# Issuing each matmul of the row maxima twice in an attention and mixture-of-experts block

## The reference

```python
q, k = _apply_rope(q, k)                                  # [8, 16, 256, 64]
scores = jnp.einsum('bhqd,bhkd->bhqk', q, k) * scale
attn = jax.nn.softmax(scores, axis=-1)
out = jnp.einsum('bhqk,bhkd->bhqd', attn, v)
...
x = _layernorm(x + attention(x))
x = _layernorm(x + experts(x))
```

## Time and profile before

| | |
|---|---|
| Median of 3 runs | 293.36 us (292.1 to 294.01) |
| Profiled execution, whole | 295.25 us |
| Span of the profiled execution, first to last instruction | 293.5 us |
| Mean granted TensorE clock in the profile | 0.819 |
| Busy in the span | PE 246.1 us, DVE 235.9 us, ACT 168.0 us, PEld 139.2 us, POOL 20.6 us |
| Matmuls | 1785, of them 256 of the row maxima (L353) |

### The profile page before, as it was taken

The page is one execution under the profiler, slowest core; times in us unless marked ns, Lnnn a source line. Parts: engine busy times, 40 slices in busy tenths (PEclk is TensorE's granted clock), DMA queues, the critical chain, the costliest instruction groups (busy, mean ns, idle before and its releaser), DMA issues.

```text
span 293.5 us, 5981 instructions
## 1 busy us (share of the span) xinstructions
PE 246.1 (84%) x1785; PEld 139.2 (47%) x1785; DVE 235.9 (80%) x688; ACT 168.0 (57%) x327; POOL 20.6 (7%) x34
## 2 busy tenths in 40 slices
PE   2737999997789789979988797999799938899991
PEld 0111345464446444645555355546545725466671
DVE  5898786969996989699798969897985794656985
ACT  3901556676858575846677574858534645545210
POOL 5000000000000000000000000000080010000121
PEclk9999999999955965685597859558855797999997
DMA  7153113030302021111113030303120000000012
GB/s 276 59 135 72 37 36 75 1 74 2 74 22 54 22 53 29 43 36 36 45 27 72 1 72 1 72 1 72 27 47 1 0 4 0 2 0 2 36 40 71
DMA packets 20438, 12.66 MB, mean 43 GB/s; under 512 B 2732, under 2 KB 19396, under 8 KB 20420
## 3 DMA queue, kind: packets, MB, share of 16 engines
q1 hardware_dynamic: 20420, 12.44, 16.5%
HBM read 2.92 MB, written 1.05 MB: 14 GB/s over the span
## 4 chain that ended last, share of the span: by engine, by line
issue 71%; PE 17%; DVE 7%; ACT 2%; POOL 2%; POOLq 0%; DVEq 0%
PE ps_o L487 4%; PE ps_s L461 3%; PE ps_t L370 2%; PE ps_s L353 2%; POOL sd L742 1%; PE ps_t L471 1%; PE ps_o L385 1%; PE ps_o L485 1%; ACT hg L715 1%; PE ps_m L448 1%; DVE qk L778 1%; DVE qk L777 1%; ACT oT_sb L651 1%; POOL rs L764 1%; PE ps_m L395 1%
## 5 line engine op out<-in xcount | busy, mean ns | idle before, releaser
L812 DVE TENSOR_REDUCE row_max<-ps_s 128x2 bf16<-128x512 f32 x128 | 86.7, 679 | 20.9 <-PE ps_s L353 19.7
L656 ACT ACTIVATE probs<-ps_t 128x512 bf16<-128x512 f32 x128 | 74.6, 606 | 35.4 <-PE ps_t L370 35.0
L353 PE MATMUL ps_s<-qk 64*128 64x256 bf16 x256 | 67.5, 359 | 7.5 <-DMA qk<-roped 4.8
L370 PE MATMUL ps_t<-qk 128*128 128x256 bf16 x256 | 66.5, 355 | 3.5 <-DMA qk<-mT_sb 1.7
L638 ACT ACTIVATE raw<-ps_m,bqk 128x256 bf16<-128x256 f32 x128 | 51.2, 478 | 9.3 <-PE ps_m L338 5.4
L385 PE MATMUL ps_o<-v_sb,probs 128*128 128x65 bf16 x512 | 46.5, 224 | 3.7 <-DVE o_sb L834 3.2
L385 PEld LDWEIGHTS ps_o<-v_sb,probs 128*128 128x128 bf16 x512 | 41.0, 121 | 16.2 <-issue 5.9
L645 ACT CAST v_sb<-ps_m 128x512 bf16<-128x512 f32 x32 | 17.5, 590 | 47.1 <-PE ps_m L345 47.1
L338 PE MATMUL ps_m<-in_b 128*128 (+1 forms) x128 | 35.3, 396 | 7.8 <-DMA in_b<-in_packed_b 4.6
L370 PEld LDWEIGHTS ps_t<-qk 128*128 128x128 bf16 x256 | 16.5, 106 | 42.3 <-issue 26.1
L834 DVE TENSOR_TENSOR o_sb<-ps_o,r_sum 128x256 bf16<-128x256 f32 x64 | 26.4, 412 | 0.1
(11 more groups left out here) (105 smaller groups left out, 222.7 us busy)
## 6 DMA issues: line engine op xcount, KB each, us to landing
qk<-roped SPq DMA_DIRECT2D x128, 64.0 KB, 2.1
out<-y_sb SPq DMA_DIRECT2D x3, 256.0 KB, 2.1
in_b<-in_packed_b SPq DMA_DIRECT2D x1, 706.0 KB, 5.9
in_f<-in_packed_f SPq DMA_DIRECT2D x1, 586.0 KB
in_b<-in_packed_b SPq DMA_DIRECT2D x1, 516.0 KB, 3.8
in_b<-in_packed_b SPq DMA_DIRECT2D x1, 512.0 KB, 4.7
x_sb<-in_x SPq DMA_DIRECT2D x1, 512.0 KB, 6.7
qk<-mT_sb SPq DMA_DIRECT2D x16, 4.0 KB, 1.7
```

The lines of the kernel that those rows point to most:

```text
L353: mm = nc.tensor.matmul(ps_s[h % 2][:, t * S:t * S + S], qk[0:DH, u % 4, 0, h, t * P:t * P + P], qk[0:DH, u % 4, 1, h, :], start=True, sto ...
L370: mm = nc.tensor.matmul(ps_t[h % 2][:, c * S:c * S + S], qk[:, u % 4, 1, h, c * P:c * P + P], qk[:, u % 4, 0, h, :], start=True, stop=True)
L656: nc.scalar.activation(probs[:, h % 4].rearrange("p c s -> p (c s)"), ps_t[h % 2][:], ACT.Exp, scale=DH ** -0.5).then_inc(exp_done, 1)
L812: nc.vector.tensor_reduce(row_max[:, u % 2, h, :], ps_s[h % 2][:].rearrange("p (t s) -> p t s", s=S), AX_X, ALU.max, negate=True).then_inc ...
```

## The change

Each head's pair of matmuls for the row maxima is issued twice, one pair behind the other, with the same operands and into the same place of the same bank. The signal to DVE is raised by the last matmul of the second pair. Each matmul starts its own accumulation (`start=True`), so the values in the bank are the same.

```diff
+MAX_TIMES = 2
...
                 need(pe, max_done, n(it, UH, u, h - 1))
-                for t in range(QT):
-                    mm = nc.tensor.matmul(ps_s[h % 2][:, t * S:t * S + S],
-                                          qk[0:DH, u % 4, 0, h, t * P:t * P + P],
-                                          qk[0:DH, u % 4, 1, h, :], start=True, stop=True)
+                for _ in range(MAX_TIMES):
+                    for t in range(QT):
+                        mm = nc.tensor.matmul(ps_s[h % 2][:, t * S:t * S + S],
+                                              qk[0:DH, u % 4, 0, h, t * P:t * P + P],
+                                              qk[0:DH, u % 4, 1, h, :], start=True, stop=True)
                 mm.then_inc(s_ready, 1)
```

## The result

| | before | changed |
|---|---|---|
| Median | 293.69 us (292.1 to 294.05, 4 runs) | 298.29 us (296.5 to 300.86, 4 runs) |
| Ratio | | 1.0174, 95% interval 1.0089 to 1.0259 |
| Profiled execution, whole / span | 295.25 / 293.5 us | 300.86 / 299.0 us |
| Mean clock as the profile gives it | 0.819 | 0.895 |
| Matmuls of the maxima | 256 | 512 |

What follows compares the result with a forecast made beforehand. TensorE was taken to bound the kernel at the low clock, VectorE at the high one. With the clock division unchanged, 4.0 + 7.7 + 23.0 = 34.7 us on the 293.36 us median gave 328 us, range 306 to 350, chance 0.72.

Steps and rivals of the forecast that it cites:

- What bounds the kernel: Whole span: TensorE sets the time at the low clock, VectorE at the high one; 0 to 64.1 us taken as low.
- The price of a matmul: Each added maxima matmul of 256 columns on 64 rows: 0.213 us at the low clock, 0.11 at the high.
- Up to 34 us: Start of the kernel, 26 maxima matmuls, partly hidden in PE's waits for DVE: 4.0 us, between 1.5 and 5.5.
- 34 to 64.1 us and the low stretches: PE full, nothing hidden: 36 matmuls cost 7.7 us, then 108 in seven low-clock stretches after 64.1 us cost 23.0.
- The signs that the prediction named: Clock checks: first rise no earlier than 74 us; mean clock far from 0.70, first rise to last maxima, would be wrong.
- I set the net at 0: Clock division between high and low: the change's opposing effects cancel, so 0 us, with bounds 307 and 347 us.
- the two pulls: Added 64-row work delays rises by diluting 128-row work at low clock, and makes falls rarer by filling PE's idle time.
- The falls: Clock drops after PE's 1.76 us wait for DVE's `attn`: rarer with idle time filled, but that wait stays.
- High stretches at 0 us: High-clock stretches after 64.1 us: 87 added matmuls covered by PE's slack under DVE, 0 us, upper bound 9.6.
- Rival 2: Clock stays high once risen because added matmuls fill PE's idle time, kernel gets faster: 286 us, chance 0.08.
- half of the low work turns high: Lower bound of the clock term, after 64.1 us: gives back half of 23.0 + 18.9, 21 us, for 307 us.
- Rival 1: Clock stays low nearly throughout, with low stretches further diluted by 64-row work: 368 us, chance 0.16.

Runs made afterwards that it cites:

- both doubled: Scores and maxima matmuls both issued twice per head, against the kernel before: 287.1 us, ratio 0.9795.
- the kernel on 128 rows: Kernel before with its maxima matmuls run once, on 128 rows in place of 64, added rows nearly all zeros: 273.41 us, ratio 0.9368.

## Why the prediction was wrong

- **What bounds the kernel: right.** TensorE at the low clock, VectorE at the high one; only the runs with three pairs and with both doubled, which load PE far more, make it pace at the high clock as well. So was reading the start as low clock against its column.
- **The price of a matmul: right.** 213 and 110 ns were forecast, 0.43 and 0.21 us per pair measured, eight added matmuls cost 1.7 us between 34 us and the second transposition of maxima, and the run with three pairs gives 196 ns.
- **Up to 34 us: mis-sized.** I took 4.0 us, between 1.5 and 5.5, and 2.3 were measured. More of it hid in PE's waits than I took.
- **34 to 64.1 us and the low stretches, 7.7 + 23.0 us: this is the step that failed.** The price was multiplied by the matmuls that ran low *before*. In the changed kernel 148 issued ones run low, so 74 added ones, 15.8 us instead of 36 for 170. The sum assumed a fixed division between clock levels, though it is made by the very stream that the change thickens. The signs that the prediction named went against it: the first rise came at 38.0 us and not at 74 or later, and the mean clock was 0.88 and not 0.70.
- **"I set the net at 0": wrong, and on evidence that I misread.** The run with three pairs, with its late rise and its long high stretch, fits the two pulls. But their sizes differ. I held that rises would come at transposes or at the output projection. The first rise of the changed kernel has maxima, scores and projections ahead of it, no more. I argued from the 30 us of full PE at the low level that maxima do not help; in a second profile of the same kernel that stretch ended at 59.2 us, and in one whose program agrees to there, at 37.5. One execution had shown the late end of a wide spread.
- **The falls: half right.** The wait for `attn` remains (7.8 us in all against 9.1). But I concluded that the falls behind it would remain as well. With more matmuls around it, a stretch of 71.7 us outlives three closings.
- **High stretches at 0 us: right for a PE with slack, too low here.** 12.6 us per unit against 12.2 (of the kernel on 128 rows, which also lacks the switches) is 0.4 us for 16 added matmuls of 1.7 us. Over the nine or so units at the high clock that makes 3 to 4 us; the forecast allowed up to 9.6.
- **Sum of what was found.** 15.8 us at the low clock less the 3.2 that the start hid (5.5 less 2.3), and 3 to 4 at the high: about 16 us of cost. The two spans differ by 5.5. So about 11 us came back from the clock. This last figure is a remainder; no run measures it by itself.
- **Rivals.** Rival 2 had the right direction (its clock that is never lowered did not come, and the kernel was not faster), the chance 0.08 and a price for its full form only. What happened lies between it and the forecast, and no case of mine had a price there: the bound for "half of the low work turns high" was 307, too high. It counted only low work behind 64.1 us, while here the first rise came 26 us earlier, and it took 4.0 us for the start. The rule of the Trainium skill behind that rival ("TensorE: Matmul & The Clock Gate", section "Why this matters for your kernels": keep TensorE busy to have the full clock) goes the right way in this trace but does not say all that counts: the run on 32 rows kept PE full for 27.3 us and had the low clock, the one on 128 rows left a third of PE idle for 116.1 us and had the high one. Rival 1 happened to neither profile; its dilution fits the first 96.9 us of the run with three pairs.

## What to carry to other kernels

Where TensorE changes between its two clock levels, don't price added or removed matmuls at the present division: ask what they do to the clock, and look at more than one execution, for the places of the changes move. Here added matmuls on 64 rows gave back less of the clock than as many on 128. If spare rows can be given values that don't change the result, such as zeros, try the matmul on all 128: here that took 6.3% off the kernel with no added matmul, by the higher clock and by the switches saved together.

## What the runs showed of the hardware

- At equal matmuls, columns and switches, the added matmuls on 128 rows (scores twice) left 48.2 us at the low clock, those on 64 rows (the change) 99.4 and 87.2. With the added pairs on 32 rows it is 153.8, with all maxima twice on 128 rows 28.5; these two also differ in their switches.
- Rows of zeros do not keep the clock down: the kernel on 128 rows has its high clock with 63 of the 64 added rows zero. Whether they count as much as others no run shows.
- PE busy for 65% of 116.1 us kept the full clock (maxima on 128 rows); PE busy for 99% of 27.3 us did not raise it (added pairs on 32 rows).
- A switch between matmuls on 32, 64 and 128 rows costs about 0.1 us: 0.53 us from one pair to the next against 0.43 without a switch at the low clock, and 0.33 against 0.22 at the high one (maxima to scores; 101.89 to 102.11 us in the kernel on 128 rows). The weight load stands right at the switch then (at 61.38 us, behind 0.41 us in which PEld did nothing), not ahead of it.
- The first rise of one program moves between executions: 64.1 and 59.2 us in the kernel before, 38.0 and 56.5 in the changed one.
